# First x transposed on TensorE, w_qkv loaded in a row, zero products ahead of the first V and of the last output products, second norm a slot nearer

## The reference: what is computed

```python
xn = layernorm(x)
qkv = xn @ w_qkv.T + b_qkv                  # 16 heads of 32, causal softmax
attn = softmax(q @ k.T / sqrt(32) + causal) @ v
a = attn @ w_out.T + b_out
h = silu(xn @ gate_w.T * gate_s) * (xn @ up_w.T * up_s)      # 1408 wide
f = h @ down_w.T * down_s
out = x + a + f
```

## Time and profile before

| | us |
|---|---|
| median of 3 runs | 1930.75 |
| the runs | 1926.81, 1930.75, 1939.71 |
| profiled execution, its own time | 1925.77 |
| its span | 1922.4 |
| TensorE busy in the span | 1858.9 (97%) |
| VectorE, ScalarE, GpSimd busy | 1505.5, 1443.0, 1264.4 |
| first matmul starts | 14.43 |
| first `scores` starts | 37.33 |

### The profile page before, as it was taken

How to read it: one execution, slowest core, us unless ns; L and a number is a source line. 1 busy time by engine, 2 the same in 40 slices (tenths; PEclk the granted TensorE clock), 3 DMA queues, 4 the chain that set the end, 5 groups by cost and what they waited for, 6 DMA issues and landing times.

```text
span 1922.4 us, 44220 instructions
## 1 busy us (share of the span) xinstructions
PE 1858.9 (97%) x14978; PEld 1220.4 (63%) x14978; DVE 1505.5 (78%) x4516; ACT 1443.0 (75%) x4263; POOL 1264.4 (66%) x1799
## 2 busy tenths in 40 slices
PE   6889999999999999999999999999999999999996
PEld 4556666666656666676666666666566666766663
DVE  4887778787787877778777787877878777787885
ACT  4786777868778787787867778687787877778684
POOL 5765857758576685766758576575666757576462
PEclk9999999999999999999999999999999999999998
DMA  9978969879797897979889798886978779687684
GB/s 227 160 158 159 186 130 194 149 159 181 132 197 144 171 168 136 196 132 190 152 155 187 133 192 134 161 159 134 189 128 169 150 140 183 131 182 138 121 163 94
DMA packets 818551, 305.93 MB, mean 159 GB/s; under 512 B 756176, under 2 KB 793168, under 8 KB 818320
## 3 DMA queue, kind: packets, MB, share of 16 engines
q1 hardware_dynamic: 796176, 240.79, 69.6%
q0 software_dynamic: 22144, 62.27, 13.0%
HBM read 55.59 MB, written 16.78 MB: 38 GB/s over the span
## 4 chain that ended last, share of the span: by engine, by line
PE 75%; DVE 11%; POOL 5%; ACT 5%; issue 2%; DMA 2%; SPq 1%; POOLq 0%; ACTq 0%; DVEq 0%
PE bank L252 75%; DVE phl L558 3%; ACT phl L458 2%; DVE bank L548 2%; DVE res L585 1%; ACT bank L466 1%; DVE xhl L700 1%; POOL ht L771 1%; DVE small L523 1%; DMA pt<-phl 1%; POOL qkp L744 1%; DVE fh L573 1%; DVE ft L568 1%; POOL att L754 0%; POOL ht L769 0%
## 5 line engine op out<-in xcount | busy, mean ns | idle before, releaser
L466 ACT ACTIVATE bank<-bank,small 128x512 f32<-128x512 f32 (+3 forms) x1024 | 516.8, 506 | 215.2 <-DVE small L548 214.6
L558 DVE SCALAR_TENSOR_TENSOR phl<-bank,small,phl 128x512 f16<-128x512 f32 (+3 forms) x1024 | 526.1, 545 | 139.3 <-ACT phl L458 136.2
L548 DVE CUSTOM_DVE_ANT_0 bank<-bank,mask 128x512 f32<-128x512 f32 (+3 forms) x1024 | 483.6, 503 | 179.9 <-PE bank L252 177.4
L458 ACT ACTIVATE phl<-bank,small 128x512 f16<-128x512 f32 (+3 forms) x1024 | 501.0, 532 | 29.6 <-DMA pt<-phl 19.0
L252 PE MATMUL bank<-xnT,wg 128*128 128x256 f16 x2816 | 365.7, 272 | 4.5 <-DVE fh L573 4.5
L252 PE MATMUL bank<-xnT,wu 128*128 128x256 f16 x2816 | 364.9, 273 | 0.0
L252 PE MATMUL bank<-xnT,wqkv 128*128 128x512 f16 x1536 | 353.4, 380 | 2.8 <-DMA xnT<-xhl 2.8
L252 PE MATMUL bank<-wd,ht 128*128 128x512 f16 x1408 | 314.5, 379 | 4.4 <-POOL ht L771 4.4
L252 PEld LDWEIGHTS bank<-xnT,wg 128*128 128x128 f16 x2816 | 263.0, 97 | 65.5 <-DVE fh L573 5.3
L252 PEld LDWEIGHTS bank<-xnT,wu 128*128 128x128 f16 x2816 | 275.6, 98 | 31.9
L252 PE MATMUL bank<-stk 96*128 96x512 f16 (+3 forms) x1024 | 244.8, 300 | 16.0 <-DVE phl L558 11.9
(11 more groups left out here) (97 smaller groups left out, 2193.1 us busy)
## 6 DMA issues: line engine op xcount, KB each, us to landing
stk<-qkp SPq DMA_DIRECT2D x768, 64.0 KB, 2.2
res<-in_x_dram POOLq DMA_DIRECT2D x64, 256.0 KB, 4.7
xin<-in_x_dram POOLq DMA_DIRECT2D x60, 256.0 KB, 3.9
out_dram<-res POOLq DMA_DIRECT2D x60, 256.0 KB, 4.2
pt<-phl SPq DMA_TRANSPOSE x512, 4.3
xin<-in_gate_dram POOLq DMA_DIRECT2D x11, 256.0 KB, 3.9
xin<-in_up_dram POOLq DMA_DIRECT2D x11, 256.0 KB, 4.6
xin<-in_down_dram POOLq DMA_DIRECT2D x11, 256.0 KB, 3.6
```

The costliest lines, as they stand in the source:

```text
L458: i = eng.activation(part(qt, j)[:, j % 2, 0], pb[:, off:off + W], ACT.Copy, scale=st_r[:, c:c + 1])
L466: i = eng.activation(pb[:, off:off + W], pb[:, off:off + W], ACT.Exp, bias=st_m[:, c:c + 1], scale=-1.0, accum_out=st_s[:, c:c + 1])
L548: i = eng.tensor_tensor_reduce(out=bk[:, off:off + W], in0=bk[:, off:off + W], in1=mask[:, 512 - W:512], scale=-(32.0 ** -0.5) / (QS * QS) ...
L558: i = eng.scalar_tensor_tensor(part(qt, j)[:, j % 2, 1], pb[:, off:off + W], st_r[:, c:c + 1], part(qt, j)[:, j % 2, 0], ALU.mult, ALU.sub ...
```

## The change

- GpSimd clears part of `pt[1]` (`zeros`) and makes a 128x128 unit matrix beside it (`unit`).
- TensorE multiplies zeros ahead of all (10 products with 512 columns), then for each tile of the first x computes four products with the unit matrix for the high part and four for the low part, into `first_bank`; ScalarE moves the high part (`first_moved`) and VectorE the low part (`first_low_moved`) from there into `xnT[0]`. After tiles 0, 1 and 2 stand another 4, 4 and 3 products of zeros.
- The scaled first tiles are made by GpSimd, between the roots, instead of VectorE. Semaphore counts shift accordingly.
- SyncE issues all twelve loads of w_qkv without waits between them; the four DMA transposes of batch 0 are gone. The two broadcast loads (`dsc`, `bout`) now stand after all of them, where before they stood ahead of chunks 8 to 11. GpSimd's wait for the last transpose ahead of its six loads is gone.
- The order on ScalarE and VectorE at the start is written anew.
- `norm_at` of batch 1 is 2, 6, 10, 14.
- At the end TensorE waits for the last low part of the probabilities (`v_lo`) and multiplies 12 times 512 columns between the last AV and the wait for its split.

```diff
-            norm_at[40 * b - 40 + 4 * t + (3 if b == 1 else 0)] = (b, t)
+            norm_at[40 * b - 40 + 4 * t + (2 if b == 1 else 0)] = (b, t)
...
-    later = [(n - (4 if n < 4 else 3), ("norm", *v)) for n, v in norm_at.items()] + [(n - 3, ("check", c)) for n, c in check_at.items()]
+    later = [(n - 3, ("norm", *v)) for n, v in norm_at.items()] + [(n - 3, ("check", c)) for n, c in check_at.items()]
...
+    zeros = pt[1][:, 0:4, :].rearrange("p a b -> p (a b)")
+    unit = pt[1][:, 4, :]
+    first_hl = [xhl[0], xhl[1], phl[3][0][:, 0], phl[3][0][:, 1]]
+    first_bank = [(bank[t], bank[4 + t % 2]) for t in range(4)]
...
+        def keep_busy(bk, count):
+            for _ in range(count):
+                mm(bk[:, :], zeros[:, 0:128], zeros[:, :], True, True)
+
+        def first_transposes(t):
+            hl = first_hl[t]
+            for p, made in enumerate(((a_xh, t + 1), (v_xl, t + 1))):
+                w.wait_ge(*made)
+                if p and t >= 2:
+                    w.wait_ge(v_xt, t - 1)
+                bk = first_bank[t][p]
+                for kt in range(4):
+                    i = mm(bk[:, 128 * kt:128 * kt + 128], hl[:, p, 128 * kt:128 * kt + 128], unit, True, True)
+                i.then_inc(s_xt, 1)
+
+        w.wait_ge(p_zero, 1)
+        keep_busy(bank[7], 10)
+        w.wait_ge(p_unit, 1)
+        for t in range(4):
+            first_transposes(t)
+            keep_busy(bank[7], (4, 4, 3, 0)[t])
         v(0, 0, 0)
...
         w.wait_ge(s_oe, 4)
+        w.wait_ge(v_lo, NU)
+        keep_busy(bank[2], 12)
         w.wait_ge(p_al, 4 * B)
...
+        first_high(0)
+        weight(0)
+        first_high(1)
+        first_moved(0)
+        weight(1)
+        first_high(2)
+        first_moved(1)
+        first_high(3)
+        first_moved(2)
+        weight(2)
+        first_moved(3)
+        for n in range(3, 7):
             weight(n)
...
         first_statistics(0)
         first_statistics(1)
-        first_scaled(0)
         first_statistics(2)
-        first_scaled(1)
         first_low(0)
         first_statistics(3)
-        first_scaled(2)
         first_low(1)
-        first_scaled(3)
+        first_low_moved(0)
         weight_low(0)
         first_low(2)
+        first_low_moved(1)
         weight_low(1)
         first_low(3)
-        for n in range(2, 7):
+        first_low_moved(2)
+        weight_low(2)
+        first_low_moved(3)
+        for n in range(3, 7):
             weight_low(n)
...
         for t in range(4):
             root(t, t)
+            w.wait_ge(p_rs, t + 1)
+            eng.tensor_scalar(x0[t], x0[t], lst[t][:, 6:7], lst[t][:, 8:9], op0=ALU.subtract, op1=ALU.mult).then_inc(p_x0, 1)
...
-        w.wait_ge(d_xT[3], 16)
         for i in range(6):
             load_ffn(i)
...
-        for t in range(4):
-            turn_x(0, t, xhl[t] if t < 2 else phl[3][0][:, t - 2])
-            load_weight(4 + t)
+        for n in range(4, NCH):
+            load_weight(n)
         for i, (dst, src) in enumerate(((dsc, down_s), (bout, b_out))):
             eng.dma_start(dst[:, :], src.to_broadcast([128, 512])).then_inc(d_small[i + 3], 16)
-        for n in range(8, NCH):
-            load_weight(n)
```

More of the change, by code:

```diff
@@ L113, in fast_path @@
     bank = [ctx.enter_context(nc.psum_tensor(f"bank{i}", [128, 512], F32)) for i in range(8)]
-    s_s, s_qk, s_v, s_av, s_o, s_gu, s_dn, s_oe, s_flag = (sem("s_" + n) for n in ("s", "qk", "v", "av", "o", "gu", "dn", "oe", "flag"))
-    a_exp, a_rec, a_hi, a_q32, a_vh, a_a32, a_ft, a_up, a_xh, a_w, a_wo, a_ms = (sem("a_" + n) for n in ("exp", "rec", "hi", "q32", "vh", "a32", "ft", "up", "xh", "w", "wo", "ms"))
+    s_s, s_qk, s_v, s_av, s_o, s_gu, s_dn, s_oe, s_xt, s_flag = (sem("s_" + n) for n in ("s", "qk", "v", "av", "o", "gu", "dn", "oe", "xt", "flag"))
+    a_exp, a_rec, a_hi, a_q32, a_vh, a_a32, a_ft, a_up, a_xh, a_xt, a_w, a_wo, a_ms = (sem("a_" + n) for n in ("exp", "rec", "hi", "q32", "vh", "a32", "ft", "up", "xh", "xt", "w", "wo", "ms"))
     v_max, v_rc, v_lo, v_fa, v_fh, v_vl, v_oy, v_dd = (sem("v_" + n) for n in ("max", "rc", "lo", "fa", "fh", "vl", "oy", "dd"))
-    v_bn, v_bna, v_var, v_xs, v_xl, v_w, v_wo, v_peak, v_most, v_chk, v_end = (
-        sem("v_" + n) for n in ("bn", "bna", "var", "xs", "xl", "w", "wo", "peak", "most", "chk", "end"))
+    v_bn, v_bna, v_var, v_xs, v_xl, v_xt, v_w, v_wo, v_peak, v_most, v_chk, v_end = (
+        sem("v_" + n) for n in ("bn", "bna", "var", "xs", "xl", "xt", "w", "wo", "peak", "most", "chk", "end"))
     p_qh, p_ql, p_ah, p_al, p_fm, p_hh, p_fl, p_res, p_dy = (sem("p_" + n) for n in ("qh", "ql", "ah", "al", "fm", "hh", "fl", "res", "dy"))
-    p_rs, p_xh, p_w, p_ne, p_set = (sem("p_" + n) for n in ("rs", "xh", "w", "ne", "set"))
+    p_rs, p_x0, p_xh, p_w, p_ne, p_zero, p_unit, p_set = (sem("p_" + n) for n in ("rs", "x0", "xh", "w", "ne", "zero", "unit", "set"))
     d_small = [sem(f"d_small{i}") for i in range(5)]
@@ L246, in xn_waits @@
         for t in tiles:
-            w.wait_ge(d_xT[t], 16 * (b + 1))
+            if b:
+                w.wait_ge(d_xT[t], 16 * b)
+            else:
+                w.wait_ge(a_xt, t + 1)
+                w.wait_ge(v_xt, t + 1)
     def tensor_program(eng):
@@ L446, in high @@
             if n < 2:
-                w.wait_ge(d_xT[2], 16)
-                w.wait_ge(d_xT[3], 16)
+                w.wait_ge(s_xt, 8)
             for j, qt, off in segs(u):
@@ L468, in exponent, with first_high, first_moved @@
             i.then_inc(a_exp, 1)
-        for t in range(4):
[L471 to L475, removed]
+        def first_high(t):
+            w.wait_ge(p_x0, t + 1)
+            eng.activation(first_hl[t][:, 0], x0[t], ACT.Copy).then_inc(a_xh, 1)
+        def first_moved(t):
+            w.wait_ge(s_xt, 2 * t + 1)
+            eng.activation(xnT[0][:, 0:4, 128 * t:128 * t + 128], first_bank[t][0][:, :].rearrange("p (a b) -> p a b", a=4), ACT.Copy).then_inc(a_xt, 1)
+        first_high(0)
[10 more added lines that the diff above has]
+        for n in range(3, 7):
             weight(n)
@@ L609, in check_end @@
             col = lambda a, b=None: most[:, a:(b or a + 1)]
-            w.wait_ge(v_xs, 4 * B)
+            w.wait_ge(v_xs, 4 * (B - 1))
             w.wait_ge(v_most, 19)
@@ L641, in first_statistics, with first_low_moved @@
             statistics(t, t, x0[t])
-        def first_scaled(t):
-            w.wait_ge(p_rs, t + 1)
-            eng.tensor_scalar(x0[t], x0[t], lst[t][:, 6:7], lst[t][:, 8:9], op0=ALU.subtract, op1=ALU.mult).then_inc(v_xs, 1)
         def first_low(t):
-            hl = xhl[t][:, :, :] if t < 2 else phl[3][0][:, t - 2]
+            hl = first_hl[t]
             w.wait_ge(a_xh, t + 1)
             eng.tensor_tensor(hl[:, 1], x0[t], hl[:, 0], ALU.subtract).then_inc(v_xl, 1)
+        def first_low_moved(t):
+            w.wait_ge(s_xt, 2 * t + 2)
+            eng.tensor_copy(xnT[0][:, 4:8, 128 * t:128 * t + 128], first_bank[t][1][:, :].rearrange("p (a b) -> p a b", a=4)).then_inc(v_xt, 1)
         first_statistics(0)
         first_statistics(1)
-        first_scaled(0)
         first_statistics(2)
-        first_scaled(1)
         first_low(0)
         first_statistics(3)
-        first_scaled(2)
         first_low(1)
-        first_scaled(3)
+        first_low_moved(0)
         weight_low(0)
         first_low(2)
+        first_low_moved(1)
         weight_low(1)
         first_low(3)
-        for n in range(2, 7):
+        first_low_moved(2)
+        weight_low(2)
+        first_low_moved(3)
+        for n in range(3, 7):
             weight_low(n)
@@ L810, in load_res @@
             eng.dma_start(res[t][:, :], x[b, 128 * t:128 * t + 128, :]).then_inc(d_res[t], 16)
+        eng.memset(pt[1][:, 0:5, :], 0.0).then_inc(p_zero, 1)
         eng.memset(mask[:, :], 0.0).then_inc(p_set, 1)
+        w.wait_ge(p_zero, 1)
+        eng.affine_select(out=unit, in_=unit, compare_op=ALU.not_equal, fill=1.0, base=0,
+                          pattern=[[-1, 128]], channel_multiplier=1).then_inc(p_unit, 1)
         eng.memset(ones[:, :], 1.0)
@@ L865, in gpsimd_program @@
                 if t >= 2:
-                    w.wait_ge(d_xT[t - 2], 16 * (b + 1))
+                    w.wait_ge(d_xT[t - 2], 16 * b)
                 elif b >= 2:
-                    w.wait_ge(d_xT[t + 2], 16 * b)
+                    w.wait_ge(d_xT[t + 2], 16 * (b - 1))
                 else:
-                    w.wait_ge(d_xT[t], 16)
-                w.wait_ge(v_xs, i + 1)
+                    w.wait_ge(s_xt, 2 * t + 2)
+                w.wait_ge(v_xs, i - 3)
                 eng.tensor_scalar(xhl[t % 2][:, 0], xin[t % 2][:, :], 1.0, 1.0, op0=ALU.mult, op1=ALU.mult).then_inc(p_xh, 1)
```

3 lines of the change are left out of this document (1 added, 2 removed).

## The result

| | before | after |
|---|---|---|
| median of 20 runs, us | 1929.69 | 1937.6 |
| range, us | 1921.13 to 1940.35 | 1930.59 to 1946.39 |
| ratio to before | | 1.0043 (95%: 1.0031 to 1.0055) |
| profiled execution, its own time | 1925.77 | 1946.39 |
| its span | 1922.4 | 1944.8 |

The changed kernel is slower by about 8 us, 0.43%. A faster one was forecast: 1919.5, range 1910 to 1929.

A forecast was written before the change was run, and what follows sets the result against it. TensorE was taken as the bound, with 63.5 us without work and lower-clock matmuls to win. 4.8 + 1.5 + 2.3 = 8.6 gave 1917.2 from the profiled execution, 1922.2 from the median; forecast the middle, 1919.5, range 1910 to 1929.

The forecast's parts named there:

- V at 14.5: Start: the first V of group 0 begins at 14.5 us, as before; about 15.5 if GpSimd's operations take 1.28 each.
- I take 0.62, the single-input row: Start: each of GpSimd's four 128x512 scaling operations takes 0.62 us, like the float16 copy.
- The upper bound of 1.28: Start: GpSimd's scaling takes 1.28 us each if like the float32 addition, putting V at about 15.5.
- One collision of 0.8 with GpSimd: Start: one VectorE low part is slowed beside GpSimd, charged 0.8 us before V; none to four possible.
- V in 2.8 us: Start: with zero products ahead, the first V takes 2.8 us instead of 4.26, so Q(0) starts 1.2 us earlier.
- From Q(0) to the scores: Start: no wait for chunk 8, `scores(0)` at 34.2, 3.1 us earlier; shorter idle keeps the next V fast, 1.7 us more.
- Second norm, a gain of 1.5: Batch 1's norm a slot nearer: shorter transposed-x wait in slot 23, less AV delay; 1.5 us, bounds loss 3, gain 4.2.
- The half credited at slot 23: Slot 23: half of the 2.8 us wait for transposed x plus 1.4 of lower clock, credited as 2.1 to 3.
- The start's gain, carried to the end whole: Start: 4.8 us won, bounds 0.5 and 6.8, entered in full in the sum for the whole kernel.
- the prediction's own last sign of being wrong: Slots 5 to 20: waits won at the start reappear as waits for VectorE, fuller than TensorE there.
- End, 2.3: End: zero products hold the clock, the last 12 matmuls take 2.7 us instead of 5.28; 2.3 us kept.
- The rival that ended slower: Slots 11 and 15: x transposes ahead of probabilities' transposes delay AV, 8.7 us each, 1938 with both jammed; chance 0.04.

The follow-up runs named there:

- scale_mult: Changed kernel with GpSimd's four first scaled tiles as x times 1.0 times 2048.0, batch 0 not normalised; one execution, the four such variants gave 1924.56 to 1939.52 us.
- x_first: Changed kernel with only the first x load of batch 1 issued ahead of the first six gate and up loads; 1933.45 us, ratio to before 1.0008.
- scale_vector: Changed kernel with the first four scaled tiles on VectorE again; 1930.22 us, ratio to before 0.9994.
- norm_only: Kernel before with only the norms of batch 1 a slot nearer; 1933.55 us, ratio to before 1.0023.
- res_spread: both_back with only the four residual loads of batch 0 moved to slots 8, 10, 12, 14 from 16 to 19; 1920.73 us, ratio to before 0.9953.
- loads_moved: both_back with the four residual loads at slots 8, 10, 12, 14 and the w_out pieces six slots later; 1924.16 us, ratio to before 0.9969.
- both_back: Changed kernel with scaled tiles on VectorE and norms of batch 1 at slots 3, 7, 11, 15 again; 1923.87 us, ratio to before 0.998.

## Why the prediction was wrong

- **V at 14.5.** Wrong: 19.20. The failed step is "I take 0.62, the single-input row" for GpSimd's scaling. That row was a mult-mult; the new operation is a subtract-mult and takes 2.1 to 2.6. The upper bound of 1.28 was an addition of two tiles and no bound for it either. Undoing the step gives 7 us by the medians. scale_mult shows it with its assumed price: V at 13.94, `scores(0)` at 32.98.
- **One collision of 0.8 with GpSimd.** It did not come. The low part at 8.28 took 0.69 with GpSimd's scaling beside it throughout. By the Trainium skill (GPSIMD Engine Reference, section 1) a two-input VectorE operation contends with GpSimd; these rows do not show it on VectorE, the 1.51 of the earlier trace rows did. In the kernel after a low part at 187.21 took 1.23 beside the subtraction of `split_qk`, so what GpSimd executes seems to matter.
- **V in 2.8 us.** Wrong in the changed kernel: 4.26. The profile shows the granted clock at 0.50 from 19.2 to 22.2, after pauses of 1.3 to 2.8 us between the bursts. With the scaling on VectorE and shorter pauses it ran in 2.78, without the zero products in 4.24. With the slow scaling and its pauses four profiles have 4.01 to 4.36, but x_first, with the same start, has 2.78: there the granted clock was at 0.50 already from 11.5 to 16.6, in the middle of the bursts, and back at 1.00 from 17.2. With such pauses it comes out either way.
- **From Q(0) to the scores.** Right. The wait for chunk 8 is gone. From the start of V to `scores(0)` it took 22.90 us before, 20.72 after and 19.34 in scale_vector; 19.7 was predicted. The pause before `scores(0)` was below 2 us, and the next V took 2.79.
- **Second norm, a gain of 1.5.** Wrong in sign: undoing it gives 7 us, doing it alone costs 4. The failed sentence is that its operations "only move by a slot on engines that are as full in the one as in the other, and are costed at nothing". The slot also fixed when VectorE needs the x tile, and the earlier trace rows were read for the transposes only. The loads took 9.04 and 7.86 us, and the first, though no slower than before (8.7), was issued 4.7 us later; on VectorE this made 6.1 us of waits, and TensorE waited for VectorE after each of them (2.37 at 54.89, 3.69 at 68.03). What was foreseen, the AV of slot 14 behind the moved transpose, came as 2.6 instead of 2 us (SyncE issues the transpose of x at 79.52 and that of the probabilities at 80.87; it lands 4.6 us later, just before the AV at 85.58, for which the profile names no releaser). The half credited at slot 23 is seen in norm_only (1.08 for 2.79). In the changed kernel that wait grew to 9.41, because transposes and GpSimd's loads met there; res_spread and loads_moved show these loads as the cause of such a wait in both_back, and for the changed kernel itself it is inferred.
- **The start's gain, carried to the end whole.** Wrong too, and, as far as one profile each can tell, it would have been with the scaling at 0.62. The sum takes the 4.8 us won up to `scores(0)` as won for the kernel. scale_mult is 4.4 ahead of before at `scores(0)` (32.98 for 37.33) and 2.0 behind at AV 2 (113.17 for 111.21), with the norm moved; both_back, with the norm in its old place, is 3.1 ahead and then 2.5 behind. Between 38 and 111 us TensorE's waits in both_back come to 17.9 us, against 11.9 before: 13.6 instead of 8.6 for VectorE, close to the prediction's own last sign of being wrong (4.24 of it stand at 104.10, where transposes were late), and 4.3 instead of 2.8 for the transposed x. A large part belongs to the loads in slots 16 to 19; with the residual loads moved (res_spread) AV 2 is 3.8 ahead of before. No timed pair shows a gain of the new start by itself beyond its interval.
- **End, 2.3.** Right: 2.76 for 5.28, a gain of 2.5 on TensorE and of 2.0 from the last AV to the end of the span.
- **The rival that ended slower** had the right stretch and the wrong queue: delays of probabilities' transposes by x's, where the larger part was VectorE waiting for a load. Its chance of 0.04 was far too low; it was priced only as a jam in both places, and the slow scaling was no rival at all.

## What to carry to other kernels

A duration may be taken from a row only if its arithmetic operations are the same too; shape, type and engine are not enough. Before a step is moved nearer, the landing time of the load that feeds it belongs in the sum, together with what stands ahead of that load in its queue. A gain at the start is worth what is left of it at the next crowded stretch (both_back: 3.1 us ahead at `scores(0)`, 2.5 behind at AV 2), so it is well to read the place of a later landmark, here the first two AV groups, in every profile.

## What the runs showed of the hardware

- GpSimd's two-operation `tensor_scalar` on 128x512 float32 takes 0.62 us as mult-mult or mult-add and 1.9 to 2.6 as subtract-mult; per-partition operands account for some 0.15 to 0.2 of it. VectorE takes 0.54 for the subtract-mult. A normalisation as x times r plus (minus mean times r) would fit the fast form; it was not tried.
- DMA transposes beside GpSimd-issued loads of 256 KB (both_back) landed after 14.8 and 18.5 us, where the median of the stretch is 4.5, with the DMA engines full at 81 GB/s, and the issue of one held SyncE for 12.1 us. With the residual loads moved away none took over 5.5.
- Executions of the same kernel differ by up to 19 us (1921.13 to 1940.35 before), and they do so together with TensorE's mean granted clock: of the executions of the kernel before that were run beside the experiments, those at 0.996 took 1925.5 us on average and those at 0.991 1934.4. Two profiled ones differ by 10 us in a stretch that the change does not touch. A difference of 2 to 5 us between versions is hard to tell from the medians, and a place in one profile can be off by as much (AV 1: 71.96 and 77.01 with the same program up to there), so it takes a sign that several profiles share.
